# Turning the experts' rows by transposing transfers, with small VectorE work moved to GpSimd, in a fused attention and mixture-of-experts kernel

## The reference

```
# attention, 8 heads of 16 channels, within each sequence of 128 tokens
xn = layernorm(x)
q, k, v = xn @ Wq + bq, xn @ Wk + bk, xn @ Wv + bv
scores = where(adj > 0, q k^T / 4, -9e15)
x = x + softmax(scores) v @ Wo + bo
# mixture of experts, 8 experts, top 2, and a shared one
y = layernorm(x)
shared = gelu(y @ W1s + b1s) @ W2s + b2s
rw = softmax(y @ Wr);  top2 of rw, renormalised -> weights of the pairs
routed = sum over the 2 chosen e of weight_e * (gelu(y @ W1p[e] + b1p[e]) @ W2p[e] + b2p[e])
x = x + shared + routed
```

## Time and profile before

| | |
|---|---|
| median of three executions | 1564.83 us (1561.16 to 1564.96) |
| the profiled execution, its own time | 1566.65 us |
| its span in the trace | 1564.8 us |
| TensorE busy | 1238.3 us (79%), 9505 instructions |
| VectorE busy | 1101.2 us (70%), 2467 |
| ScalarE busy | 984.6 us (63%), 1713 |
| GpSimd busy | 876.4 us (56%), 922 |
| mean busy share of the DMA engines over the span | the page's row "DMA": 1 to 2 tenths in the attention phase, 2 to 5 in the expert phases |

### The profile page before, as it was taken

How to read it: one execution, slowest core, us unless ns; L and a number is a source line. 1 busy time by engine, 2 the same in 40 slices (tenths; PEclk the granted TensorE clock), 3 DMA queues, 4 the chain that set the end, 5 groups by cost and what they waited for, 6 DMA issues and landing times. The chain is left out here.

```text
span 1564.8 us, 33624 instructions
## 1 busy us (share of the span) xinstructions
PE 1238.3 (79%) x9505; PEld 706.7 (45%) x9506; DVE 1101.2 (70%) x2467; ACT 984.6 (63%) x1713; POOL 876.4 (56%) x922
## 2 busy tenths in 40 slices
PE   2999999999999999837899977888888888878300
PEld 1566666666666666623344433333443333334100
DVE  3688898888899888845677764555565555555288
ACT  1677777777777777625677766676776767667200
POOL 3246666666666666536756652556565656555500
PEclk9999999999999999968899998999999999999755
DMA  2012222122222211122354322333233333333099
GB/s 59 28 55 64 68 67 65 62 65 63 65 67 67 66 62 47 42 68 75 109 147 126 115 62 51 72 65 79 67 74 67 75 69 77 67 67 80 10 333 312
DMA packets 225698, 128.33 MB, mean 82 GB/s; under 512 B 128175, under 2 KB 203998, under 8 KB 225644
## 3 DMA queue, kind: packets, MB, share of 16 engines
q1 hardware_dynamic: 191596, 85.44, 21.6%
q0 software_dynamic: 17408, 33.87, 6.4%
q10 hardware_dynamic: 16640, 8.39, 1.8%
HBM read 47.37 MB, written 55.09 MB: 65 GB/s over the span
## 5 line engine op out<-in xcount | busy, mean ns | idle before, releaser
L935 DVE SCALAR_TENSOR_TENSOR h<-hid,h 128x512 f16<-128x512 f32 x416 | 286.1, 693 | 265.6 <-ACT h L915 223.3
L1224 POOL DMA_INDIRECT pairs_dram<-x_rows x288 | 294.1, 1021 | 104.1 <-issue 104.0
L915 ACT ACTIVATE h<-hid 128x512 f16<-128x512 f32 x416 | 261.9, 630 | 57.8 <-remote 10.6
L887 PE MATMUL Y<-h,w 128*128 128x512 f16 x1248 | 292.0, 384 | 7.1 <-DVE h L935 4.4
L876 PE MATMUL Z<-x_rows,w 128*128 128x512 f16 x864 | 209.8, 395 | 93.0 <-issue 76.3
L926 ACT ACTIVATE hid<-Z,biases 128x512 f32<-128x512 f32 x416 | 279.8, 673 | 0.0
L887 PEld LDWEIGHTS Y<-h,w 128*128 (+1 forms) x1248 | 122.5, 99 | 163.9 <-issue 22.3
L419 DVE TENSOR_REDUCE smax<-S 128x8 f32<-128x1024 f32 x128 | 155.8, 1217 | 47.4 <-PE S L642 47.4
L1029 POOL DMA_INDIRECT slots_dram<-x_rows,pair_slot x140 | 143.4, 1024 | 70.5 <-issue 40.6
L876 PEld LDWEIGHTS Z<-x_rows,w 128*128 x864 | 81.8, 101 | 201.0 <-issue 121.5
L422 DVE TENSOR_TENSOR probs<-S,smax 128x1024 f32<-128x1024 f32 x128 | 156.8, 1225 | 16.1 <-DVE smax L419 3.4
(11 more groups left out here) (165 smaller groups left out, 2092.5 us busy)
## 6 DMA issues: line engine op xcount, KB each, us to landing
y_pairs<-pairs_dram SPq DMA_DIRECT2D x32, 512.0 KB, 6.0
x_res<-in_x_dram SPq DMA_DIRECT2D x32, 256.0 KB, 3.2
adj<-in_adj_dram SPq DMA_DIRECT2D x32, 256.0 KB, 3.0
x_rows<-x SPq DMA_DIRECT2D x32, 256.0 KB
xT_dram<-xT SPq DMA_DIRECT2D x32, 256.0 KB
xTu<-xT_dram SPq DMA_DIRECT2D x32, 256.0 KB
out_dram<-x_res ACTq DMA_DIRECT2D x16, 512.0 KB, 10.1
pairs_dram<-x_rows POOLq DMA_INDIRECT x288
```

The costliest lines, as they stand in the source:

```text
L887: mm = pe.matmul(self.Yt[:, b], self.w2[:, m, :, c][:, e, :], self.h16[:, b, k, c], start=c == 0 and n == 0, stop=c == FC - 1 and n == 2)
L915: act.activation(self.h16[:, b, 0, c], self.hid[:, c], ACT.Copy, scale=HS).then_inc(self.hi_done, 1)
L935: dve.scalar_tensor_tensor(out=self.h16[:, b, 1, c], in0=self.hid[:, c], scalar=HS, in1=self.h16[:, b, 0, c], op0=ALU.mult, op1=ALU.subtra ...
L1224: pool.indirect_dma_start(pairs_dram, bass.IndirectOffsetOnAxis(ap=pair_of[n][:, j:j + 1], axis=0), y_sb[n % NIN][:, j], None, bounds_chec ...
```

## The change

Four edits:

1. The task `x2T` goes from PE and ScalarE. SP issues four transposing transfers per group instead (`turn_rows`), each from one tile of `x16` in SBUF (128 x 256 f16, 64 KB) to its place in `xT`, after `keep_rows` of the group. `lg`, `store_xT` and the next group's write of `x16` wait for their landing (`x2T_in`).
2. The mask moves from VectorE to GpSimd, between the two paced scatters.
3. `ve1` and `ve2` move from VectorE to GpSimd, ahead of the powers that read them, with a wait between the two.
4. The running totals are kept as f16 counts in units of 128 inside `pick` (column GT), and PE adds them in the rank product: `RANK` loses its fifth column, and one product by `ones` takes the counts. VectorE then needs three instructions in `place`, not four: `eq`, the count, and a sum that writes the integer slots at once. The router phase starts from the same counts, with three more products on PE and four fewer instructions on VectorE (two of them over 128 x 1024).

The diff, cut to its core:

```diff
@@ sync engine
         def store_xT(g, q):
-            wait(sp, "x2T_sb", g + 1)
+            wait(sp, "x2T_in", (g + 1) * GT * 16)
...
+        def turn_rows(g, q):
+            for j in range(GT):
+                sp.dma_start_transpose(xT[:, q, :, j * P:(j + 1) * P], x16[:, j].rearrange("p a c -> p (a c)"))\
+                    .then_inc(s["x2T_in"], 16)
...
             keep_rows(2 * r - 5)
+            turn_rows(2 * r - 5, 1)
@@ GpSimd
         def norm1(g, q):
-            wait(pool, "ln1_stats", g + 1)
+            wait(pool, "aggr1", g + 1)
             wait(pool, "xT_ps", g)
-            pool.tensor_tensor(rs1[:, q], ve1[:, q], half[:], ALU.pow).then_inc(s["rs1_done"], 1)
+            pool.tensor_scalar(ve1[:], mv1[:, q, :, 1], EPS, None, ALU.add).then_inc(s["ve1_done"], 1)
+            wait(pool, "ve1_done", g + 1)
+            pool.tensor_tensor(rs1[:, q], ve1[:], half[:], ALU.pow).then_inc(s["rs1_done"], 1)
...
         def split(g):
...
+            pool.tensor_scalar(ve2[:], mv2[:, :, 1], EPS, 1.0 / (XS * XS), ALU.add, ALU.mult).then_inc(s["ve2_done"], 1)
...
-            wait(pool, "x2T_ps", g)
+            wait(pool, "x2T_in", g * GT * 16)
+            wait(pool, "lg_ps", g - 1)
+            if g >= 2:
+                pool.wait_ge(xT_stored[g % 2], g // 2 * 16)
             wait(pool, "rows_kept", 16 * g)
...
+        def mask(g, q):
+            pool.wait_ge(adj_loaded[q], (g // 2 + 1) * 16)
+            wait(pool, "s_ps", (g - 1) * GT)
+            pool.tensor_scalar(negmask[:, q], adj[:, q], 0.0, NEG, ALU.is_le, ALU.mult).then_inc(s["mask_ready"], 1)
...
             if late:
                 scatter(g - 5, 0, g * GT)
+            if has(g, -1):
+                mask(g + 1, (g + 1) % 2)
+            if late:
                 scatter(g - 5, 1, g * GT + 1)
@@ VectorE
             wait(dve, "on_ps", turned)
-            wait(dve, "ranked", g + 1)
-            dve.tensor_tensor(rt.run[:, q], RANK, rt.run[:, 1 - q, GT].unsqueeze(1).to_broadcast([P, GT + 1, E]),
-                              ALU.add).then_inc(s["ranked"], 1)
-            wait(dve, "ranked", g + 2)
-            dve.tensor_tensor(eq[:], rt.run[:, q, 0:GT], pick[:, q, 0:GT], ALU.mult).then_inc(s["slot_terms"], 1)
+            dve.tensor_tensor(eq[:], RANK, pick[:, q, 0:GT], ALU.mult).then_inc(s["slot_terms"], 1)
+                dve.tensor_reduce(count[:, 1 - q], pick[:, q].rearrange("p j e -> p e j"), AX_X, ALU.add).then_inc(s["counted"], 1)
+            set_up(dve, g)
             wait(dve, "slot_terms", g + 1)
-            dve.tensor_reduce(slot_f[:], eq[:], AX_X, ALU.add).then_inc(s["slot_sum"], 1)
-            set_up(dve, g)
-            wait(dve, "slot_sum", g + 1)
-            dve.tensor_copy(rt.pair_slot[:, bass.ds(g * GT, GT), 0], slot_f[:]).then_inc(s["slot_ready"], 1)
+                dve.tensor_reduce(rt.pair_slot[:, bass.ds(g * GT, GT), 0], eq[:], AX_X, ALU.add).then_inc(s["slot_ready"], 1)
@@ ScalarE
-            elif task == "x2T":
-                wait(act, "x2T_ps", g + 1)
...
-                act.activation(xT[:, q], M16, ACT.Copy).then_inc(s["x2T_sb"], 1)
@@ TensorE
-            elif task == "x2T":
-                wait(pe, "split_done", g + 1)
...
-                        mm = pe.transpose(M16[:, part, j * P:(j + 1) * P], x16[:, j, part], ident16[:])
...
             elif task == "lg":
-                wait(pe, "x2T_sb", g + 1)
+                wait(pe, "x2T_in", (g + 1) * GT * 16)
...
-            pe.matmul(RANK, rt.before[:], pick[:, q], start=True, stop=False)
-            for j in range(GT):
-                mm = pe.matmul(RANK[:, j + 1:GT + 1], rt.ones[:], pick[:, q, j].unsqueeze(1).to_broadcast([P, GT - j, E]),
-                               start=False, stop=j == GT - 1)
+            pe.matmul(RANK, rt.before[:], pick[:, q, 0:GT], start=True, stop=False)
+            pe.matmul(RANK, rt.ones[:], pick[:, q, GT].unsqueeze(1).to_broadcast([P, GT, E]), start=False, stop=False)
+            for j in range(GT - 1):
+                mm = pe.matmul(RANK[:, j + 1:GT], rt.ones[:], pick[:, q, j].unsqueeze(1).to_broadcast([P, GT - 1 - j, E]),
+                               start=False, stop=j == GT - 2)
@@ router phase, TensorE and VectorE
+            pe.matmul(R_tiles[:, b * NT // 2:(b + 1) * NT // 2], rt.ones[:], counts1.unsqueeze(1).to_broadcast([P, NT // 2, E]),
+                      start=False, stop=False)
...
-        then(dve.tensor_tensor(eq, pick2, over_tiles(first_totals), ALU.mult))
-        then(dve.tensor_reduce(base_slot[:], eq, AX_X, ALU.add))
```

More of the change, by code:

```diff
@@ L35 @@
 REGION = NT * P + UT
+assert REGION % P == 0 and (E - 1) * REGION // P + NT <= 2048
 BLANK = E * REGION
@@ L69, in attention_phase @@
     key = sb("key", [P, GT])
-    slot_f = sb("slot_f", [P, GT])
-    pick = sb("pick", [P, 2, GT + 1, E], F16)
+    pick = rt.pick
+    count = pick[:, :, GT]
     qb = sb("qb", [P, 1])
@@ L96, in attention_phase @@
     mv2 = sb("mv2", [P, GT, 2])
-    ve1 = sb("ve1", [P, 2, GT])
+    ve1 = sb("ve1", [P, GT])
     ve2 = sb("ve2", [P, GT])
@@ L306, in scatter @@
                                     row_words[:, g * GT + j, :], None).then_inc(row_sent[j], 16)
+        mask(0, 0)
         norm1(0, 0)
@@ L370, in gather1 @@
             last.then_inc(s["aggr1"], 1)
-            wait(dve, "aggr1", g + 1)
-            dve.tensor_scalar(ve1[:, q], mv1[:, q, :, 1], EPS, None, ALU.add).then_inc(s["ln1_stats"], 1)
-        def mask(g, q):
-            dve.wait_ge(adj_loaded[q], (g // 2 + 1) * 16 if isinstance(g, int) else (g - q) * 8 + 16)
-            wait(dve, "s_ps", (g - 1) * GT if isinstance(g, int) else g * GT - GT)
-            dve.tensor_scalar(negmask[:, q], adj[:, q], 0.0, NEG, ALU.is_le, ALU.mult).then_inc(s["mask_ready"], 1)
         def residual(g):
@@ L400, in gather2 @@
             last.then_inc(s["aggr2"], 1)
-            wait(dve, "aggr2", g + 1)
-            dve.tensor_scalar(ve2[:], mv2[:, :, 1], EPS, 1.0 / (XS * XS), ALU.add, ALU.mult).then_inc(s["ln2_stats"], 1)
         def normalise(t, g, q, j):
@@ L467, in step @@
                 gather1(0, 0)
-                mask(0, 0)
                 stats1(1, 1)
@@ L477, in step @@
                     stats2(g - 2)
-                if j == 3 and has(g, -1):
-                    mask(g + 1, 1 - q)
                 if has(t, 0, NT):
@@ L541, in step @@
                 t = g * GT + j
-                b = {0: ("x2T", g - 4, q), 1: ("aT", g - 2, q), 2: ("xT", g + 1, 1 - q), 3: ("K", g + 1, 1 - q)}[j]
+                b = {0: None, 1: ("aT", g - 2, q), 2: ("xT", g + 1, 1 - q), 3: ("K", g + 1, 1 - q)}[j]
                 a = {0: ("lg", g - 4, q), 1: None, 2: ("Q", g + 1, 1 - q), 3: ("V", g + 1, 1 - q)}[j]
-                if has(b[1]):
+                if b and has(b[1]):
                     evac(*b)
@@ L560, in _ @@
         pair_blocks(act, step)
-        evac("x2T", NG - 1, (NG - 1) % 2)
         evac("lg", NG - 1, (NG - 1) % 2)
@@ L597, in m0_task @@
                 mm.then_inc(s["out_ps"], 1)
-            elif task == "x2T":
-                wait(pe, "split_done", g + 1)
-                m0_free(pe, task, step_g)
-                for part in range(2):
-                    for j in range(GT):
-                        mm = pe.transpose(M16[:, part, j * P:(j + 1) * P], x16[:, j, part], ident16[:])
-                mm.then_inc(s["x2T_ps"], 1)
             elif task == "lg":
-                wait(pe, "x2T_sb", g + 1)
+                wait(pe, "x2T_in", (g + 1) * GT * 16)
                 m0_free(pe, task, step_g)
@@ L783, in _ @@
                               start=False, stop=c == (CH if b else CH // 2) - 1)
+        pe.matmul(totals, rt.ones[:], counts1, start=True, stop=False)
         for c in range(CH):
-            mm = pe.matmul(totals, counts[:, c], rt.later[:, NT * E:(NT + 1) * E], start=c == 0, stop=c == CH - 1)
+            mm = pe.matmul(totals, counts[:, c], rt.later[:, NT * E:(NT + 1) * E], start=False, stop=c == CH - 1)
         mm.then_inc(ranks_ps, 1)
@@ L813, in _ @@
         dve.tensor_copy(counts, chunk_counts.unsqueeze(2).to_broadcast([P, CH, P])).then_inc(counts_sb, 1)
-        dve.wait_ge(pick2_ready, 1)
-        then(dve.tensor_tensor(eq, pick2, over_tiles(first_totals), ALU.mult))
-        then(dve.tensor_reduce(base_slot[:], eq, AX_X, ALU.add))
         dve.wait_ge(ranks_ps, 1)
         then(dve.tensor_tensor(eq, R_tiles, pick2, ALU.mult))
-        then(dve.tensor_reduce(slot_f[:], eq, AX_X, ALU.add))
-        then(dve.tensor_tensor(rt.pair_slot[:, :, 1], slot_f[:], base_slot[:], ALU.add))
-        then(dve.tensor_tensor(rt.tot[:], totals, first_totals, ALU.add))
+        with nc.allow_low_precision(reason="whole numbers below 2 ** 24"):
+            then(dve.tensor_reduce(rt.pair_slot[:, :, 1], eq, AX_X, ALU.add))
+        then(dve.tensor_copy(rt.tot[:], totals))
 class Ffn:
```

42 lines of the change are left out of this document (22 added, 20 removed).

## The result

On the chips of the first measurement the changed kernel took 1571.4 us (median of 20 executions, 1567.4 to 1578.1) and the kernel before 1564.9 (20 executions, 1559.5 to 1570.3): ratio 1.0047, 95% interval 1.0033 to 1.0060. It is 0.5% slower where 0.9% faster was forecast. The same two kernels on another chip gave 0.9894 (0.9879 to 0.9908). Both numbers hold; the experiments say what lies between them. The profiled execution of the changed kernel took 1571.56 us, its span 1569.7.

A forecast was written before the change was run, and what follows sets the result against it. PE was taken to bound S(1) to S(3), VectorE or both engines S(3) to S(1). 1566.65 - 17.5 (loop) + 3 (drain) = 1552.15, or 1550.3 us on the median's scale; own range 1544 to 1558, 8 in 10 1540 to 1562.

The forecast's parts named there:

- leg A: Attention loop, S(1) to S(3) of a group, 10.17 us: held by PE, to stay at 10.2 us.
- covered: GpSimd's added work, 1.3 us a group and 2 at most, costs nothing, as 5.5 us of idle less 0.6 hides it.
- Leg B: Attention loop, S(3) to S(1): 9.98 us falls to 9.18, 9.49 to 9.05; mean saving 0.62 us a group.
- the 0.8 I took: VectorE's `place` in the attention loop falls from 1.66 to 0.85 us, saving 0.8 us (0.66 to 0.96).
- x2T alone: PE is free of x2T 0.55 us earlier, but ON waits for `oT`, so 0.34 us survive.
- swallowed: Rival: PE holds S(3) to S(1) in both kinds of group; 9.5 us won, 5 to 6 lost in the drain: 1561, chance 0.14.
- VectorE's large names: Taking `ve2` and the mask off VectorE, ahead of the maximum of tile 3, saves nothing, as PE holds that stretch.
- The mask: On GpSimd, between the paced scatters, it takes 0.8 us; with the small instructions and waits 1.3 us, 2 at most.
- the transfers hold the loop: Rival: SP's four transposing transfers outlast each group; 1.7 us a group at 5 us each, about 50 us slower: 1615, chance 0.08.
- The prediction's estimate: Drain of the attention phase: by a fixed part of about 2 us each, four in series take 8.6 us, drain near +6.
- the drain: End of the attention phase: the last groups wait for the transfers, net 0.5 to 7 us, taken as +3.
- the phases behind: Router phase costs 0, within 0.5 us; later phases 0.

The follow-up runs named there:

- e2: Kernel before with only the rows turned by four transposing transfers in place of x2T, chip 6: ratio 1.0000 to the kernel before.
- e3: Kernel before with only the running count moved into the rank product, chip 6: ratio 0.9950 to the kernel before.
- e12: Kernel before, unaltered, one execution traced on chip 12: group 19.91 us.
- e1: Changed kernel with the rows turned on PE again in place of the transfers, chip 6: ratio 1.0010 to the kernel before.
- e16: Changed kernel with `ve1` and `ve2` on VectorE again, chip 1: ratio 0.9951 to the kernel before.
- e4: Changed kernel with the mask on VectorE again, chip 6: ratio 1.0034 to the kernel before.
- e15: Changed kernel, unaltered, chip 1: ratio 1.0029 to the kernel before.
- e9: Kernel before with the count in the rank product, scatter(0) let go by S(1) and scatter(1) by S(2), chip 13: ratio 0.9935 to the kernel before.
- e5: Changed kernel with `ve1` and `ve2` on VectorE again, chip 13: ratio 0.9904 to the kernel before.
- e10: Changed kernel with scatter(0) let go by S(1) in place of S(0), chip 13: ratio 0.9912 to the kernel before.
- e11: Changed kernel, unaltered, chip 12: ratio 0.9894 to the kernel before.
- e17: Changed kernel with scatter(0) let go by S(1) in place of S(0), chip 1: ratio 0.9918 to the kernel before.
- e14: Changed kernel with scatter(0) let go by S(1) in place of S(0), chip 12: ratio 0.9903 to the kernel before.

## Why the prediction was wrong where it was wrong

*The step that failed* is the one on leg A: "S(3) has no wait ahead: PE holds this leg", with the condition "I am wrong if leg A moves by more than 0.3 us". It moved by +0.65 in the mean. PE does hold the leg, but through the signals of its own products: `aT` to ScalarE, `attnT` back to `out`, S(1) to the maximum. I took a product as usable at the end of its row and had no term for what else decides that.

*Why the pair meets S(1) now.* From the moment GpSimd has xT to the end of scatter(0) is a fixed chain of GpSimd alone: 320.16 to 333.82 in the trace of before, 13.66 us, and 13.67 in e2, e3 and e12. With `ve1` and `ve2` in it the chain is 14.31 (322.62 to 336.93), and 14.33 in e1. So these two small instructions with their waits cost 0.65 us on it, more than my 0.4 to 0.6, and I called the cost covered, since GpSimd idles ahead of `norm1`. The idle is real but lies ahead of the chain's start, which waits for PE; behind that start every instruction moves the pair. PE needs 14.5 us from the end of xT to the end of S(1) (15.05 before in the kind with the branch). The hold ends about 0.8 us behind scatter(0): at 0.16 + 13.66 + 0.8 = 14.6 before, just when S(1) ends, and at 15.3 now, 0.8 us too late, which is what the trace shows. e3 meets it from the other side: there the chain is unchanged and S(1) ends earlier. The traces with the hold agree throughout (medians): where scatter(0) is over 0.7 us or more before S(1) ends, S(1) is 0.2 us late at most (before, e2, one kind of e3 and e16); at 0.3 us it is 0.33 and 0.55 late (the other kinds of e3 and e16); where both end together, 0.6 to 0.9 (e1, e4, e15, the changed kernel).

*Leg B.* Forecast -0.62 us in the mean, found -0.36 with the hold and -0.27 without. `place` fell from 1.66 to 0.50 us, more than the 0.8 I took, and the kind of group with the branch reached 9.11 in e3 against my 9.18. The other kind was mis-sized: I had PE at 9.05 to 9.15, and PE needs 9.4 to 9.5, since with S earlier it waits for ScalarE: 0.48 for the first half of PT, as forecast, 0.27 in one kind for `oT`, and 0.3 to 0.4 for K's evacuation ahead of V (0.20 in one kind before), which I did not count. The 0.34 us that I gave to x2T alone had a wait wrong too: I let ON wait for `oT` only, and e2 shows it waiting for `attn` behind `place`, so that without edit 4 nothing is left of it. The "swallowed" rival was nearer here. Without the hold leg A fell by 0.20, which I did not have either and no run takes apart (e9, with edit 4 and the pace alone, has it too), so the group fell by 0.45, and 27 groups by 12 us where I had 17.5.

*VectorE's large names* gave back nothing, as forecast: e5 and e10 agree within 0.1 us a group, and VectorE waits about 0.86 us for S(3) (e11). More than that: e9 has edit 4 and the pace alone, with the mask and both `ve` on VectorE and x2T on PE, and its group takes 19.48 us against the 19.46 of the changed kernel and the 19.91 of the kernel before, all without the hold. The pace moves nothing there (e10 and e11), so edit 4 makes nearly the whole gain of the loop, and edits 1 to 3 next to none of it.

*GpSimd.* The mask takes 1.95 us, where I took 0.8 with 2 us as the most for all of it. The Trainium skill (GPSIMD Engine Reference, Engine selection) calls one input roughly line-rate; the trace does not agree: a cast over as many elements takes 0.61 us, this comparison with a product 1.95, and in the kernel before VectorE took 0.41 for the same mask. It cost the time nothing (e4: the group is 0.06 longer without it), for it stands behind the pair and ahead of the wait for PE.

*The transfers.* Four take 5.17 us of SP's queue, 1.29 each, at the upper of my bounds (1.36 for one of four times the size), and land 2.7 to 2.9 us after their issue began. In the loop they were free (e2); "the transfers hold the loop" falls. The prediction's estimate by the Trainium skill (DMA: Bandwidth & Descriptors, Anatomy of one DMA — SWDGE (gpsimd) path: a fixed part of about 2 us for each transfer) was 8.6 us for `keep_rows` and four in series; the trace has 7.4, from the issue of `keep_rows` at 314.30 to the last landing at 321.67, the issues following each other every 1.3 us and the landings overlapping. In the drain `lg` waits 6.46 and 5.97 us, and the attention phase ends 8.3 us later after the last S; on chip 12 it is 7.2, and in e15, the same kernel, only 3.9 more than in the trace of before. My 0.5 to 7 was too low for two of the three. Against that the phases behind had slack that I put at nothing: in the kernel before VectorE stood 3.83 us at the barrier ahead of the router phase, now 0.33 (it also has three instructions fewer there, not four). From the last S to the copy that closes the router phase it is 59.3 us against 55.3, on chip 12 57.7 against 54.8, and 54.9 in e15. So +4.0 and +2.9, the forecast +3; but one kernel spreads over 4.4 us here, and two misses that cancel, the drain and the barrier, make the agreement luck.

*The sum.* With the hold: loop +7.5 us (last S at 667.9, before 660.4), drain and router +4.0, and 6.6 fewer in the later phases. Without: -11.9, +2.9, and 8.5 fewer. No edit touches the later phases, and no run explains those last terms. From the router's closing copy to the end it takes 842 to 855 us in the traces with the hold and 814 to 822 in those without, so one trace settles no 6 us. It also means that my 1550.3 would have been nearly right without the hold as a ratio (0.991 against 0.9894), but by luck: 5.6 us too much gain in the loop, and 8.5 behind the router that I did not have.

## What to carry to other kernels

- Idle time of an engine covers an added instruction only if it lies behind it in the same chain. Idle ahead of the chain's start, which another engine sets, covers nothing: what is added behind that start moves everything that the chain ends in, here two scatters by 0.65 us.
- Compare the end of a product with the start of its first user. Where they lie apart and the user has no other wait, look for indirect transfers issued close together beside it, and move them by one wait: letting scatter(0) go by S(1) made a 0.3% loss a 0.8% gain on a chip that holds (e15 and e17), and cost nothing that could be told on one that doesn't (0.9903 in e14 against 0.9894 in e11). That version beats the kernel before on three chips, and the changed kernel on the one of them that holds.
- A change of under 1% is worth measuring on more than one chip. Here its sign depends on it.

## What was not expected of the hardware

- Two kinds of chip. In the first measurement and on chips 6 and 1, completion signals of PE come up to 2.2 us late beside two successive indirect transfers of GpSimd; on 12 and 13, with the same instructions at the same distances, none in the loop is over 0.08. The kernel before takes 1565 to 1570 us on the former and 1535 to 1537 on the latter; of that 30 us only 2.5 stand ahead of the copy that closes the router phase (715.7 against 713.2). What makes a chip one or the other no run shows.
- A transposing transfer from SBUF costs SP's queue 1.29 us for 64 KB and 1.38 for 256 KB; a copy from SBUF to SBUF 0.68 us for 256 KB and for 2 KB.
- A cast to integers in a reduction of VectorE (`pair_slot`, 0.18 us) waits for no instruction of GpSimd, though one with two inputs runs beside it in all 20 groups from 200 to 600 us; the plain cast took 0.72.
